# Twenty expert steps moved four steps forward in a fused attention and MoE kernel, with its last copies and additions rearranged

## What is computed

```python
xn = layernorm(x)                                   # x: 2 x 2048 tokens, 128 wide
# attention
s = xn @ W_spin.T + b_spin
scores = (s @ W_J.T) @ s.T / sqrt(128)              # 2048 x 2048 for each of the two batches
local = softmax(scores) @ s
attn = tanh(beta * (s + mean(s) @ W_global.T + local))
# mixture of experts: 16 experts, the best 2 of each token
top_vals, top_idx = top_k(xn @ Wg.T + bg, 2); rw = softmax(top_vals)
gu = xn @ Wgu[e] + bgu[e]; gate = min(gu[::2], 7); up = clip(gu[1::2], -7, 7)
out_e = ((up + 1) * gate * sigmoid(1.702 * gate)) @ Wd[e] + bd[e]
ffn = sum over the 2 experts of rw * out_e
result = x + attn + ffn
```

## Time and profile before

| | |
|---|---|
| median of 3 runs | 374.11 us (373.42 to 375.37) |
| the profiled execution | 375.0 us, its span 373.2 us |
| TensorE busy | 328.0 us (88%) |
| VectorE busy | 306.4 us (82%) |
| ScalarE busy | 256.1 us (69%) |
| GpSimd busy | 217.2 us (58%) |
| 64 scatters (line 458) | 62.4 us busy, 19.8 us idle before them |
| 64 gathers (line 488) | 34.5 + 32.3 us busy, 20.4 + 9.7 us idle before them |
| mean granted TensorE clock | 0.975 of full speed |

### The profile page before, as it was taken

One profiled execution on the slowest core, in us unless ns is written; L12 is line 12 of the kernel. 1 busy time (PEld: TensorE's weight loads), 2 busy tenths in 40 slices (PEclk: granted clock), 3 DMA queues, 4 the chain that ended last, 5 costly groups with the idle time before them and its releaser, 6 DMA issues.

```text
span 373.2 us, 5903 instructions
## 1 busy us (share of the span) xinstructions
PE 328.0 (88%) x1773; PEld 272.7 (73%) x1773; DVE 306.4 (82%) x607; ACT 256.1 (69%) x509; POOL 217.2 (58%) x247
## 2 busy tenths in 40 slices
PE   2769799897999999999997999999979999997930
PEld 1547588664778788888876999999858777786720
DVE  4896877999978969969966998899798989967862
ACT  4955866674588787687683788888746776696820
POOL 5606798122577779777723345344207877777771
PEclk9997999999999999999999999999999999999985
DMA  5999600000011210212133477686453354565541
GB/s 149 327 320 365 245 4 2 0 1 30 7 50 59 75 57 26 88 49 79 57 93 91 134 235 231 203 242 207 143 171 101 98 141 128 133 142 134 124 131 56
DMA packets 41359, 45.97 MB, mean 123 GB/s; under 512 B 3770, under 2 KB 33082, under 8 KB 41330
## 3 DMA queue, kind: packets, MB, share of 16 engines
q1 hardware_dynamic: 36162, 32.94, 28.4%
q0 software_dynamic: 5168, 12.67, 12.0%
HBM read 23.46 MB, written 22.12 MB: 122 GB/s over the span
## 4 chain that ended last, share of the span: by engine, by line
POOL 37%; PE 24%; DVE 14%; issue 12%; DMA 5%; ACT 4%; SPq 1%; POOLq 0%; DVEq 0%; ACTq 0%
POOL slots_x L458 16%; POOL made L488 9%; POOL gy L488 8%; PE PS L497 4%; PE PS L499 4%; PE PS L498 4%; DVE mx L1014 4%; DMA xy<-slots_x 2%; DVE pl L999 2%; PE PS L722 2%; PE PS L604 2%; PE PS L707 2%; PE PS L551 1%; POOL rows L449 1%; PE PS L724 1%
## 5 line engine op out<-in xcount | busy, mean ns | idle before, releaser
L856 ACT ACTIVATE PS<-PS 128x512 f32<-128x512 f32 x128 | 74.8, 584 | 53.0 <-PE PS L499 51.1
L999 DVE TENSOR_TENSOR pl<-PS,ph 128x512 fp32r<-128x512 f32 x128 | 87.6, 685 | 24.8 <-ACT ph L867 24.1
L1014 DVE TENSOR_REDUCE mx<-PS 128x1 f32<-128x512 f32 x128 | 84.2, 681 | 8.7 <-PE PS L551 8.5
L867 ACT ACTIVATE ph<-PS 128x512 fp32r<-128x512 f32 x128 | 76.5, 598 | 12.4 <-ACT PS L856 0.7
L458 POOL DMA_INDIRECT slots_x<-xn,posu x64 | 62.4, 975 | 19.8 <-issue 18.9
L551 PE MATMUL PS<-xT,gq 128*128 128x512 f32 x128 | 49.1, 422 | 8.2 <-DVE mx L1014 7.8
L497 PE MATMUL PS<-ph,rows 128*128 128x512 f32 x128 | 51.6, 403 | 4.0 <-DVE pl L999 3.8
L497 PE MATMUL PS<-gq,xT 128*128 128x512 f32 x128 | 52.5, 410 | 1.3 <-DVE pl L999 1.3
L499 PE MATMUL PS<-gq,xT 128*128 128x512 f32 x128 | 50.1, 392 | 0.0
L499 PE MATMUL PS<-ph,rows 128*128 128x512 f32 x128 | 50.1, 391 | 0.0
L498 PE MATMUL PS<-pl,rows 128*128 128x512 f32 x128 | 50.0, 391 | 0.0
(11 more groups left out here) (188 smaller groups left out, 687.7 us busy)
## 6 DMA issues: line engine op xcount, KB each, us to landing
slots_y<-yr SPq DMA_DIRECT2D x20, 512.0 KB, 3.2
slots_x<-xs SPq DMA_DIRECT2D x1, 5120.0 KB, 21.8
xy<-slots_x SPq DMA_DIRECT2D x20, 256.0 KB, 3.0
xn<-in_L_attn_x SPq DMA_DIRECT2D x8, 256.0 KB, 5.2
w_f<-in_L_ffn_Wgu SPq DMA_DIRECT2D x1, 2048.0 KB, 12.9
late<-in_L_ffn_Wgu SPq DMA_DIRECT2D x1, 2048.0 KB, 18.3
xs<-in_L_attn_x SPq DMA_DIRECT2D x8, 256.0 KB, 3.3
out_y<-made SPq DMA_DIRECT2D x7, 256.0 KB, 3.1
```

Source lines behind the costliest of these rows:

```text
L856: A(S[:, n % 3], S[:, n % 3], ACT.Exp).then_inc(exp_done, 1)
L867: A(ph[:, i % RING], S[:, n % 3], ACT.Copy).then_inc(s_hi, 1)
L999: v.tensor_tensor(dst, S[:, n % 3], high.bitcast(F32), ALU.subtract).then_inc(s_lo, 1)
L1014: v.tensor_reduce(mx4[:, a, c:c + 1], MX[:, n % 2], AX.X, ALU.max).then_inc(mx_free, 1)
```

## The change

The expert phase now interrupts attention between steps 75 and 76, that is after 12 of the 16 tiles of superblock 4. The accumulator of these 12 tiles is kept in a new tile `oT_part`, and `fields(4, h)` adds two products for each part. The queries of superblock 6 are made in step 63. Four scores (76 to 79) are made among the last groups. GpSimd copies the weights in quarters of the tokens, and the low parts of `rows[1]` are made by VectorE in steps 44 to 47. The results of the last group are multiplied out by ScalarE in its step 78. The additions of superblocks 0 to 6 follow the loop's steps four steps earlier, with a seventh set inside the loop; those of the last superblock are all taken after its last gathers, ahead of `combine(7, 0)` and `combine(7, 1)`, and its accumulator, Tanh and last addition are split in halves.

```diff
-    MOE_AT = 5 * TB
+    MOE_AT = 5 * TB - 4
...
         def query_at(i):
+            if i in (4 * TB - 1, 4 * TB + 12):
+                return 6 if i == 4 * TB - 1 else None
             return i // TB + 2 if i % TB == 12 and i // TB + 2 < NSB else None
...
-                    if isinstance(g, int) and g >= NG:
-                        sp.wait_ge(y_last, 2 * (g - NG) + 2)
+                    if isinstance(g, int) and g == NG:
+                        sp.wait_ge(y_last, 2)
+                    elif isinstance(g, int) and g == NG + 1:
+                        sp.wait_ge(y_ready, 2 * NG - 2)
...
-                    for k in range(CB, NCH):
-                        t = 4 * (k - CB)
-                        pool.wait_ge(row_h[1], k - CB + 1)
-                        g.tensor_tensor(rows[1][:, 1, t:t + 4, 1:D], xn[:, TB + t:TB + t + 4, 1:D],
-                                        rows[1][:, 0, t:t + 4, 1:D].bitcast(F32), ALU.subtract)
                     g.memset(rows[1][:, 0, :, 0:1].bitcast(F32), 1.0)
                     g.memset(rows[1][:, 1, :, 0:1].bitcast(F32), 0.0).then_inc(row_l[1], 1)
-                    pool.wait_ge(scat[0], 16 * NT)
                 pool.wait_ge(routed, c + 1)
-                g.tensor_copy(xn[:, :, 0], w12[:, c]).then_inc(weights_in, 1)
-                pool.wait_ge(weights_in, c + 1)
-                for t in range(NT):
-                    pool.indirect_dma_start(slots_x, bass.IndirectOffsetOnAxis(ap=posu[:, c, t:t + 1], axis=0),
-                                            xn[:, t], None).then_inc(scat[c], 16)
+                for q in range(4):
+                    if c:
+                        pool.wait_ge(scat[0][q], 16 * NT // 4)
+                    part = slice(q * NT // 4, (q + 1) * NT // 4)
+                    g.tensor_copy(xn[:, part, 0], w12[:, c, part]).then_inc(weights_in, 1)
+                    pool.wait_ge(weights_in, 4 * c + q + 1)
+                    for t in range(part.start, part.stop):
+                        pool.indirect_dma_start(slots_x, bass.IndirectOffsetOnAxis(ap=posu[:, c, t:t + 1], axis=0),
+                                                xn[:, t], None).then_inc(scat[c][0 if c else q], 16)
...
-                o = e_bank("F", k, h)
+                if (k, h) == (7, 1):
+                    pe.wait_ge(cr_done, NSB)
+                o = MX[:, 0] if (k, h) == (7, 1) else e_bank("F", k, h)
...
+                    if k == MOE_AT // TB:
+                        mm(o[:, a * w:(a + 1) * w], oT_part[:, q], AE[:, b], start=True, stop=False)
...
-                    if i == MOE_AT - 2:
-                        pe.wait_ge(cr_done, MOE_AT // TB + 1)
-                    turn_slots(i % 2, i % 2, i % 2 + 1)
+                    pe.wait_ge(mx_free, 16 * (MOE_AT // TB + 1) + 15 + i % 2)
+                    turn_slots(i % 2, 1 - i % 2, i % 2 + 1)
...
             down(NG - 1, 1, columns[NG - 1])
+            score(MOE_AT + 3)
...
+                if i == MOE_AT + 2:
+                    y_copy(NG - 1, 1)
                 if j == 13 and k + 1 < NSB:
                     shift_in(k + 1)
...
-            values_hi(4)
+            act.wait_ge(pv_done, MOE_AT)
+            A(oT_part[:], O[:, MOE_AT // TB % 2], ACT.Copy).then_inc(part_kept, 1)
...
-            values_hi(7)
-            squash(7)
+            act.wait_ge(pv_done, STEPS)
+            for h in range(2):
+                A(oT[:, 256 * h:256 * h + 256], O[:, 1, 256 * h:256 * h + 256], ACT.Copy).then_inc(o_kept, 1)
+            for h in range(2):
+                act.wait_ge(e_free, e_no["F", 7, h] + 1)
+                f = field[:, NT - 4 + 2 * h:NT - 2 + 2 * h]
+                A(f, f, ACT.Tanh, scale=betac[:]).then_inc(tanh_ready, 1)
...
+            def second_rows_lo(c):
+                t = 4 * c
+                dve.wait_ge(row_h[1], c + 1)
+                v.tensor_tensor(rows[1][:, 1, t:t + 4, 1:D], xn[:, TB + t:TB + t + 4, 1:D],
+                                rows[1][:, 0, t:t + 4, 1:D].bitcast(F32), ALU.subtract).then_inc(row_l[1], 1)
+
+            ROWS_AT = {44: 0, 45: 1, 46: 2, 47: 3}
             ADD_X_AT = {40: 0, 54: 1, 66: 2, 78: 3, 94: 4, 110: 5, 126: 6}
-            BOTH_AT = {MOE_AT + 11 + 6 * k: k for k in range(6)}
-            PARTS_AT = {MOE_AT + 12 + 6 * k: k for k in range(6)}
-            FINISH_AT = {MOE_AT + 13 + 6 * k: k for k in range(6)}
+            BOTH_AT = {MOE_AT + 11 + 6 * k: k for k in range(7)}
+            PARTS_AT = {MOE_AT + 12 + 6 * k: k for k in range(7)}
+            FINISH_AT = {MOE_AT + 13 + 6 * k + 2 * (k == 6): k for k in range(7)}
...
             prob_lo(MOE_AT + 1)
-            y_copy(NG - 1, 1)
...
             prob_lo(STEPS - 1)
-            add_both(6)
-            add_parts(6)
-            finish(6)
+            dve.wait_ge(gat_last, 64)
+            for h in range(2):
+                dve.wait_ge(gat_half[h], 32)
+            dve.wait_ge(ld_x[7], 32)
+            m = made[:, 3]
+            link(v.tensor_tensor(m, m, gy[:, 1], ALU.add))
+            link(v.tensor_tensor(m[:, :, 0:D], m[:, :, 0:D], m[:, :, D:2 * D], ALU.add))
+            link(v.tensor_tensor(m[:, :, 0:D], m[:, :, 0:D], xs[:, 1], ALU.add))
             combine(7, 0)
             combine(7, 1)
-            dve.wait_ge(gat_last, 64)
-            dve.wait_ge(ld_x[7], 32)
-            m = made[:, 3]
-            link(v.tensor_tensor(m[:, :, 0:D], m[:, :, 0:D], m[:, :, D:2 * D], ALU.add))
-            link(v.tensor_tensor(m[:, :, 0:D], m[:, :, 0:D], xs[:, 1], ALU.add))
-            dve.wait_ge(tanh_ready, NSB)
-            link(v.tensor_tensor(m[:, :, 0:D], m[:, :, 0:D], field[:, NT - 4:NT], ALU.add))
             for h in range(2):
                 t = slice(2 * h, 2 * h + 2)
-                dve.wait_ge(gat_half[h], 32)
-                link(v.tensor_tensor(m[:, t, 0:D], m[:, t, 0:D], gy[:, 1, t, 0:D], ALU.add))
-                v.tensor_tensor(m[:, t, 0:D], m[:, t, 0:D], gy[:, 1, t, D:2 * D], ALU.add).then_inc(fin_ready, 1)
+                dve.wait_ge(tanh_ready, NSB + h)
+                v.tensor_tensor(m[:, t, 0:D], m[:, t, 0:D], field[:, NT - 4 + 2 * h:NT - 2 + 2 * h], ALU.add).then_inc(fin_ready, 1)
```

More of the change, by code:

```diff
@@ L178, in build @@
         oh_ready, routed, eid_ready, route_done = sem("oh_ready"), sem("routed"), sem("eid_ready"), sem("route_done")
-        scat = [sem("scat0"), sem("scat1")]
+        scat = [[sem(f"scat0_{q}") for q in range(4)], [sem("scat1")]]
         weights_in, w_kept, ones_in = sem("weights_in"), sem("w_kept"), sem("ones_in")
@@ L315, in _ @@
                 tokens_in(4)
-                for c in range(2):
-                    sp.wait_ge(scat[c], 16 * NT)
+                for s in scat[0]:
+                    sp.wait_ge(s, 16 * NT // 4)
+                sp.wait_ge(scat[1][0], 16 * NT)
                 sp.wait_ge(s_fill, s_no["X", CB * TB - 1] + 1)
@@ L624, in values @@
                     pe.wait_ge(o_kept, k - 1)
-                if j == 0 and k in (5, 6):
-                    pe.wait_ge(y_ready, 2 * NG - 4)
-                    pe.wait_ge(y_last, 4)
+                if i == MOE_AT:
+                    pe.wait_ge(y_ready, 2 * NG - 3)
+                if i == 5 * TB:
+                    pe.wait_ge(y_ready, 2 * NG - 2)
                 if k == 0 and j % 4 == 0:
@@ L630, in values @@
                 if k == CB and j == 0:
-                    pe.wait_ge(row_l[1], 1)
+                    pe.wait_ge(row_l[1], 5)
                 pe.wait_ge(s_lo, s_no["X", i] + 1)
                 m = three(O[:, k % 2], rows[b][:, 0, j], rows[b][:, 1, j], ph[:, i % RING], pl[:, i % RING],
-                          start=j == 0, stop=j == TB - 1)
+                          start=j == 0 or i == MOE_AT, stop=j == TB - 1 or i == MOE_AT - 1)
                 m.then_inc(pv_done, 1)
@@ L647, in fields @@
             def fields(k, h):
-                o = e_bank("F", k, h)
+                if (k, h) == (7, 1):
+                    pe.wait_ge(cr_done, NSB)
+                o = MX[:, 0] if (k, h) == (7, 1) else e_bank("F", k, h)
                 b = k // CB
-                pe.wait_ge(o_kept, k + 1)
+                pe.wait_ge(o_kept, k + 1 + (k == 7 and h))
                 pe.wait_ge(e_free, e_no["M", b] + 1)
@@ L653, in fields @@
                     w, q = D + 2, slice((2 * h + a) * P, (2 * h + a + 1) * P)
-                    m = mm(o[:, a * w:(a + 1) * w], oT[:, q], AE[:, b], start=True, stop=True)
+                    if k == MOE_AT // TB:
+                        mm(o[:, a * w:(a + 1) * w], oT_part[:, q], AE[:, b], start=True, stop=False)
+                    m = mm(o[:, a * w:(a + 1) * w], oT[:, q], AE[:, b], start=k != MOE_AT // TB, stop=True)
                 m.then_inc(e_fill, 1)
@@ L658, in step @@
                 k, j = divmod(i, TB)
-                if not MOE_AT <= i < MOE_AT + 3:
+                if not MOE_AT <= i < MOE_AT + 4:
                     score(i)
@@ L756, in _ @@
             gate_up(0, columns[0])
+            pe.wait_ge(t_lo, rows_fill(1) + 1)
```

(8 more changed lines are left out.)

8 lines of the change are left out of this document (4 added, 4 removed).

## The result

The changed kernel takes **376.32 us** (median; 375.13 to 378.75) against 374.11 us of the kernel before: ratio **1.0064**, 95% interval 1.0043 to 1.0084. The profiled execution took 377.45 us with a span of 375.7 (before 375.0 and 373.2), so profile and rounds agree on about 2.5.

A forecast was written before the change was run, and what follows sets the result against it. The prediction took GpSimd's two lists of indirect DMAs, and what lies between and behind them, to bound the kernel. It summed -2.65 + 1.3 + 1.8 + 3.25 + 4.4 = +8.1 us onto 374.11, forecasting 382.2 us, range 377.5 to 386.0.

The forecast's parts named there:

- slots ready (scatters): GpSimd's scatters into the expert slots end sooner: -4.95 for the pause, +1.6 for breaks, +0.7 for contention, together -2.65 us.
- first turn to first product, without the clock: TensorE from first turned slots to first expert product: second turn waits for VectorE behind a combine, +1.3 us (0 to 2).
- clock: TensorE at the start of the experts: a 4.8 us wait for slots halves its clock for a time, +1.8 us (0 to 3.4).
- last landing to last addition: VectorE behind the last gather's landing: additions, combines and half Tanh now start only there, +4.4 us (4.0 to 5.2).
- last addition to the end: Kernel's close: silently taken to follow the last addition at a constant distance, 0 us.
- -4.95: GpSimd between the two runs of scatters: us saved by removing the four subtractions there.
- Rival (a): TensorE at the experts' start: the clock holds, all else as forecast without the 1.8, 380.4 us; chance 0.20.
- Prelude: TensorE between first turned slots and first expert product: VectorE's combine delays the second turn, +1.3 us (0 to 2).
- late copy: ScalarE's copies of the last results stand behind a shift row, exponent and high part, so the store goes +3.25 us later.
- Rival (c): Gathers at the end: they close ranks, no longer lengthened by VectorE's additions, up to 6.0 us back, 371.5 to 372.8; chance 0.07.
- (b): End of attention: it ends last as TensorE drops to 1.2 GHz while VectorE waits, about +3.5 us, 385.7; chance 0.06.
- (d): GpSimd's scatters: breaks cost 0.8 each, so scatters end +0.55 and alone set the experts' start, 385.4 us; chance 0.06.

The follow-up runs named there:

- e1: Changed kernel with the old order of the last additions (both combines first, gathered pieces as they come); ratio 1.0066 to the kernel before.
- e3: Changed kernel with ScalarE's copies of the last results one step sooner and the old order of the last additions; ratio 0.9949 to the kernel before.
- e4: Kernel before with only the change's new end of the last superblock (halved accumulator, Tanh, last addition, new order of additions); ratio 1.0021.
- g1: Kernel before with only the first choice's scatters counting on four semaphores instead of one, all four waited for; ratio 1.0041.
- g3: Kernel before with only the four subtractions moved from GpSimd to VectorE in steps 44 to 47; ratio 0.9993.
- e2: Changed kernel with ScalarE's copies of the last results one step sooner, ahead of the shift row; ratio 0.9968 to the kernel before.
- f6: Changed kernel with GpSimd's old scatters: subtractions on GpSimd and one copy of the weights for each group; ratio 1.0162 to the kernel before.
- g4: f8 with old whole weight copies and semaphores, one wait for the first run's landings, no subtractions on GpSimd; ratio 0.9907 to the kernel before, median 370.28 us.
- f5: Changed kernel with step 74's field parts ahead of the first turn of slots on TensorE; ratio 1.0038 to the kernel before.
- f8: Changed kernel with early copy, old order of last additions, field parts first, and one weight copy for the first choice; ratio 0.9934 to the kernel before, median 371.14 us.
- h1: g4 with one semaphore for the scatters of both choices instead of two; ratio 0.9851 to the kernel before, from few runs, median 369.91 us.
- h2: Kernel before with the first choice's scatters counting on eight semaphores instead of one; ratio 1.0017.

## Why the prediction was wrong, point by point

| Term of the sum | forecast | measured |
|---|---|---|
| slots ready (scatters) | -2.65 | -4.07 |
| first turn to first product, without the clock | +1.3 | +1.45 |
| clock | +1.8 | 0 in this profile; 0.25 in e1 and e3 |
| expert steps | 0 | +0.6 |
| last product to store | +3.25 | +3.22 |
| store to first gather | 0 | +0.05 |
| first gather to last landing | 0 | -0.12 |
| last landing to last addition | +4.4 | +4.38 |
| last addition to the end | 0 | **-3.0** |
| sum | +8.1 | +2.5 |

**The end.** This is the largest of three terms that together put the time outside the range; had this one, the clock or the scatters alone come out as forecast, 376.32 would have been 377.7 to 379.3 and inside it. The prediction read the last chain as ending at the last addition and took the remaining 5.46 us for a fixed close. They were 2.4 us of store and 3 us of waiting for GpSimd's drain. The tail's own 4.38 was forecast within 0.02 and was still worth little: e1, e3 and e4 put it at 0 to 1.1 us. In the kernel before, the last landing was never a link of the binding chain; that went through the last gather instruction and the drain, and of my terms only those ahead of the gathers were on it. The semaphores, which I had costed at nothing, add 1.3 us to that second way (g1). In the changed kernel the two ways end almost together, at 374.9 and 375.3, so that taking the new tail away (e1) uncovers the drain and brings next to nothing.

**The scatters.** The direction and the -4.95 were right; breaks cost 0.19 and not 0.27 each, 0.5 us in all. The contention of the four subtractions was put at 0.7, and only one of them stretched a scatter, by 0.18 (the one at 139.34). The other stretched scatter, by 0.40 at 127.36, met an addition of x (line 1187) that met none before, while the 1.47 of before is gone; the net of all is 0.1. That the four fell so well is luck: in g3, on another beat, three of them stretched a scatter, by 1.16 in all. That makes -3.7 to the last scatter, against -3.97 measured. As the slots came sooner than forecast, TensorE's wait was 3.19 and not 4.8.

**The clock.** Rival (a), that the clock holds, came true in the profiled execution: after 3.19 us of waiting TensorE still had 1.00, where 2.97 us had been followed by 0.50 at 26 us. But that was luck. e1, e2 and e3 run the same instructions up to here. In e2 a wait of 3.41 us kept 1.00; in e1 and e3 waits of 3.38 and 3.35 were followed by a granted clock of 0.50 from 190 to 193. So a wait of some 3 us loses the clock in one execution and not in the next, and neither its length nor the dense work ahead of it (25.95 us busy of the 26 before the wait) decides it by itself. What does, no run told. The step that failed is the reading of one row as a threshold, and with it the size of the term. In e1 and e3 the lost clock lengthened the way from first turn to first product by 0.25 us (5.91 and 5.93 against 5.66). In f6, after 6.94 us, it cost 0.9, and in g4, after 2.79, also 0.9 (5.49 against the 4.58 of f5, f8 and h1, which kept it after 2.84, 2.72 and 2.55). In no profile did it cost the 1.8 that was forecast. A wait of 4.8 us was not tried; in f6 the granted clock was 1.00 until 190 and 0.69 from 190 to 191, so it fell some 4.5 us into the wait.

**Prelude and late copy.** Both were right in mechanism and size, and f5 and e2 take each away: 1.08 us of the prelude come back with the field parts moved, and 3.32 with the copies moved. The expert steps took 0.6 longer. That is no more than they vary by: over the sixteen profiles they take 75.7 to 77.0 us from first to last product, at full clock in all, and the changed kernel has the longest.

**The gathers.** Rival (c) did not happen: the mean of the 32 into `made` went from 1.078 to 1.055 us, 0.7 in all, and the last landing moved by 0.12 only. The rivals (b) and (d) did not happen either: attention's field parts were there before the last landing, and the breaks were cheap. Attention's cover is smaller than forecast, though: its accumulator is complete at 364.7, 7.6 later than before and not 5.5, which leaves 3.3 us to the last landing where there were 10.

## What to carry to other kernels

Before costing anything behind the last compute instruction, look at which engine the closing barrier waited for: an engine that ends in a long drain gives every other engine cover, and edits beyond it are worth only what exceeds that cover. In this kernel the last indirect DMA on GpSimd sets the earliest end, 8.0 us behind it, so what brings that instruction forward pays and what stands beside it may not. A single profile cannot say whether a wait costs the clock: look at the same place in several. An engine's in-order queue decides what a moved step costs: the same four copies were worth 3.3 us more one step sooner, because a wait of another engine's stood ahead of them. Where an early start and an early supply are two edits, neither alone brings much (f6, which also has the late copy and the new tail, was at 1.0162, g3 at 0.9993), so judge them as a pair.

## What the runs showed of the hardware

**GpSimd's closing drain** ends 8.0 us after its last indirect DMA instruction ends, and 9.3 us with five or nine semaphores for the scatters in place of two. By the profile it starts at 344 to 352 us, while about a dozen gather instructions are still to be made, so its duration of 23.4 to 25.5 us is not what it costs. Nor does it only wait for the last gather to land: that gather has landed 6.1 us before the drain ends in the kernel before, and 7.1 in the changed one. No other engine's drain took over 0.9 us, but for TensorE's in h2 (1.28).

**Where VectorE meets an indirect DMA.** g3 shows it cleanly. Its subtractions on VectorE (start, us):

```profile
132.96 0.68 DVE L1182 TENSOR_TENSOR rows<-xn,rows 128x508 fp32r<-128x508 f32 x1
135.10 0.68 DVE L1182 TENSOR_TENSOR rows<-xn,rows 128x508 fp32r<-128x508 f32 x1
136.77 0.68 DVE L1182 TENSOR_TENSOR rows<-xn,rows 128x508 fp32r<-128x508 f32 x1
138.41 0.68 DVE L1182 TENSOR_TENSOR rows<-xn,rows 128x508 fp32r<-128x508 f32 x1
```

and its scatters on GpSimd:

```profile
135.27 1.34 POOL L453 DMA_INDIRECT slots_x<-xn,posu  x1 [0.30 <-issue]
136.91 1.37 POOL L453 DMA_INDIRECT slots_x<-xn,posu  x1 [0.30 <-issue]
138.59 1.33 POOL L453 DMA_INDIRECT slots_x<-xn,posu  x1 [0.30 <-issue]
```

A scatter that starts 0.14 to 0.18 after the start of such a subtraction is stretched from 0.96 to 1.33 to 1.37. That is what was left of the subtraction (0.50 to 0.54) less 0.13. The one at 132.96 began while a scatter was under way, and none near it is stretched. So it is the start of the indirect DMA that has to wait, and what counts is whether it falls inside the VectorE instruction. The gathers show the same. In the profiles before and after, 22 scatters and gathers start inside an addition or subtraction with two SBUF inputs, over 0.02 us behind its start and over 0.16 ahead of its end; every one is stretched by what is left less 0.12 to 0.15. Of those that start within 0.02 of each other, some are stretched and some are not. In g3, 73 start inside a VectorE instruction with at most one SBUF input, and none of them is stretched by over 0.06. The Trainium skill, page "SBUF — State Buffer", section "Who interferes with whom", infers that such an instruction, with two SBUF inputs, leaves descriptor generation alone; these rows show otherwise for an indirect DMA. Whether what waits is the generation itself or the reading of the row numbers from SBUF, no run tells.
